# Late work moved to the end of VectorE's attention slot in a macaron block

## What is computed

```python
x = x + 0.5 * ffn(layernorm(x))
x = x + attn(layernorm(x))
x = x + 0.5 * ffn(layernorm(x))

def attn(x, Q, K, VO):                      # 16 heads, rank 64
    xq = einsum('btd,hrd->bthr', x, Q)
    xk = einsum('bud,hrd->buhr', x, K)
    p = softmax(einsum('bthr,buhr->bthu', xq, xk) / sqrt(128), axis=3)
    return einsum('bthu,bud,hde->bte', p, x, VO)

def ffn(x):                                 # 3 blocks, dequantized weights + LoRA
    h = x
    for blk in range(3):
        y = gelu(layernorm(linear(h, 2 * blk)) * gamma + beta)
        h = linear(y, 2 * blk + 1) + h
    return h
```

## Time and profile before

| what | us |
|---|---|
| median of 3 runs (lowest, highest) | 1020.96 (1019.09, 1021.09) |
| the profiled execution, its own time | 1021.44 |
| its span, first to last instruction | 1019.3 |
| TensorE busy in the span | 961.0 |
| VectorE busy | 887.4 |
| GpSimd busy | 826.2 |
| ScalarE busy | 808.5 |

### The profile page before, as it was taken

The page is one execution under the profiler, slowest core; times in us unless marked ns, Lnnn a source line. Parts: engine busy times, 40 slices in busy tenths (PEclk is TensorE's granted clock), DMA queues, the critical chain, the costliest instruction groups (busy, mean ns, idle before and its releaser), DMA issues.

```text
span 1019.3 us, 19252 instructions
## 1 busy us (share of the span) xinstructions
PE 961.0 (94%) x5892; PEld 499.6 (49%) x5892; DVE 887.4 (87%) x1782; ACT 808.5 (79%) x1343; POOL 826.2 (81%) x912
## 2 busy tenths in 40 slices
PE   4897799999999999999999999999999999999897
PEld 4664244444444444444444444444444444444675
DVE  7678998998999899989998999899989988995566
ACT  4875579878888888888888978897889788878674
POOL 2646389889898999899989998999889988899552
PEclk9998899999999999999999999999999999999999
DMA  9000323233222322222233223222222232321002
GB/s 245 1 2 0 83 60 63 57 64 64 55 60 60 64 62 63 63 63 63 63 63 63 63 62 64 57 63 57 62 58 63 57 66 62 65 57 27 2 1 83
DMA packets 71742, 59.87 MB, mean 59 GB/s; under 512 B 11168, under 2 KB 70560, under 8 KB 71648
## 3 DMA queue, kind: packets, MB, share of 16 engines
q1 hardware_dynamic: 71392, 58.31, 26.4%
q10 hardware_dynamic: 256, 0.39, 0.2%
HBM read 6.23 MB, written 2.10 MB: 8 GB/s over the span
## 4 chain that ended last, share of the span: by engine, by line
PE 71%; DVE 19%; issue 4%; ACT 3%; POOL 2%; DMA 1%; DVEq 0%; SPq 0%; ACTq 0%; POOLq 0%
PE ps L1156 9%; PE ps L1158 9%; PE ps L1157 9%; PE ps L1148 8%; PE ps L1149 8%; PE ps L1141 5%; DVE mcol L900 5%; PE ps L1086 3%; PE ps L1175 3%; PE ps L1133 3%; PE ps L1058 3%; PE ps L1171 2%; PE ps L1172 2%; DVE head_ops L911 2%; PE ps L1135 2%
## 5 line engine op out<-in xcount | busy, mean ns | idle before, releaser
L455 POOL TENSOR_TENSOR p_lo<-work_b,p_hi 128x1024 f16<-128x1024 f32 x256 | 539.8, 2129 | 76.3 <-ACT p_hi L610 74.0
L900 DVE TENSOR_REDUCE mcol<-ps 128x2 f16<-128x1024 f32 x256 | 301.0, 1220 | 0.7 <-PE ps L1141 0.6
L605 ACT ACTIVATE work_b<-ps,exp_scale 128x1024 f32<-128x1024 f32 x256 | 271.6, 1111 | 33.3 <-PE ps L1149 31.9
L610 ACT ACTIVATE p_hi<-work_b 128x1024 f16<-128x1024 f32 x256 | 256.1, 1055 | 0.0
L1148 PE MATMUL ps<-head_ops 128*128 128x512 f16 x512 | 195.0, 381 | 1.1 <-DVE mcol L900 1.1
L1156 PE MATMUL ps<-p_hi,xn_hi 128*128 128x512 f16 x512 | 194.8, 380 | 0.4 <-DVE pair_ops L889 0.4
L1149 PE MATMUL ps<-head_ops 128*128 128x512 f16 x512 | 194.9, 381 | 0.0
L1158 PE MATMUL ps<-p_lo,xn_hi 128*128 128x512 f16 x512 | 194.1, 379 | 0.0
L1157 PE MATMUL ps<-p_hi,xn_lo 128*128 128x512 f16 x512 | 194.1, 379 | 0.0
L464 POOL TENSOR_TENSOR x<-x,o_sb 128x512 f32<-128x512 f32 x128 | 162.7, 1271 | 6.5 <-DVE o_sb L928 2.1
L911 DVE STREAM_TRANSPOSE head_ops<-mcol 32x128 f16<-32x128 f16 x512 | 155.4, 303 | 9.3
(11 more groups left out here) (131 smaller groups left out, 1390.9 us busy)
## 6 DMA issues: line engine op xcount, KB each, us to landing
head_ops<-pair_ops SPq DMA_DIRECT2D x512, 64.0 KB, 2.0
head_ops<-pair_ops SPq DMA_DIRECT2D x128, 128.0 KB, 2.4
x<-x_dram SPq DMA_DIRECT2D x8, 256.0 KB, 6.1
out<-x SPq DMA_DIRECT2D x8, 256.0 KB, 2.6
vo_last<-wvo_dram SPq DMA_DIRECT2D x1, 1024.0 KB, 11.9
qk<-wq_dram SPq DMA_DIRECT2D x1, 512.0 KB, 5.3
qk<-wk_dram SPq DMA_DIRECT2D x1, 512.0 KB, 6.1
scl<-scales_dram ACTq DMA_DIRECT2D x8, 48.0 KB, 5.5
```

What stands on the lines that cost most here:

```text
L455: pool.tensor_tensor(p_lo[:, k % 2, rows, :], p32[:, k % 2, rows, :], p_hi[:, k % 2, rows, :], ALU.subtract).then_inc(plo_done, 1)
L605: nc.scalar.activation(p32[:, k % 2, 2 * a:2 * a + 2, :], s_ps[a], ACT.Exp, scale=exp_scale[:, 0:1]).then_inc(exp_done, 1)
L610: nc.scalar.activation(p_hi[:, k % 2, 2 * a:2 * a + 2, :], p32[:, k % 2, 2 * a:2 * a + 2, :], ACT.Copy).then_inc(phi_done, 1)
L900: nc.vector.tensor_reduce(mcol[:, pair % 2, :, t, 0], s_ps[t % 2], AX.X, ALU.max, negate=True).then_inc(max_red, 1)
```

## The change

One line moves. In VectorE's `slot(k)`, the call of `late(k)` stood between the two `reduce_max` and `y_low(k)`; it now stands at the end of the slot, behind `y_low(k)` and `k_low` or `q_low`. The other engines' programs are as they were.

```diff
--- before
+++ after
@@ -953,7 +953,6 @@
                 if -4 <= k < NH - 4:
                     for a in range(2):
                         reduce_max((k + 4) // 2, 2 * (k % 2) + a)
-                late(k)
                 if k == NH - 1:
                     seed(1, 0)
                     seed(1, 1)
@@ -970,6 +969,7 @@
                         k_low(pair, buf)
                     else:
                         q_low(pair, buf)
+                late(k)
 
             for k in SLOTS:
                 slot(k)
```

## The result

The changed kernel takes 1034.1 us (median, 1034.07 to 1035.61) against 1020.17 us for the kernel before, run beside it: ratio 1.0136, 95% interval 1.0122 to 1.0149, so 13.9 us slower. Slower was forecast, with 1039.0 and a range of 1031 to 1049. The profiled execution took 1035.61 us with a span of 1033.5, 14.2 more than the span before.

A forecast was written before the change was run, and what follows sets the result against it. TensorE was taken to set the pace. Removed `y_low` waits -14.2, readers +27.9, bn_stats +1.3 and seeds +2.6 sum to +17.6 us, on 1021.4 giving 1039.0 us; range 1031 to 1049.

The forecast's parts named there:

- What bounds it: Attention stage: TensorE sets the pace, busy 100.98 of 103 us at granted clock 1.00; only what makes it wait counts.
- Readers of late_ps, +27.9: `outputs` waits for moved step_x_half or split: 14 x 0.95, 6 x 0.96 and 6 x 1.47 us, +27.9.
- The two parts of the offset: Reader starts at +1.32 after the start of `y_low`; its result reaches TensorE 0.06 us after its end.
- Waits for y_low removed, -14.2: Third matmul of `outputs` (line 1175) no longer waits for `y_low` at 14 seeds: 13.3 and 0.93, booked -14.2 us.
- Seeds at the end, +2.6: A lone seed, 0.74 us, delays the second reduce_max; TensorE waits 0.32 in 8 slots, +2.6 us.
- The 2.05 end of the range: Upper end for the seed's first tensor_scalar at the slot's end, taken as 0.24 us with ends 0.24 and 2.05.
- the rival in which GpSimd still holds the seeds: GpSimd holds the ports by add_out or late p_lo; seeds cost 19.5 instead of 2.6, 1055.9 us; chance 0.08.
- as the order said: GpSimd's next instruction, the Newton step, needs the seed, so in queue order it issues nothing before it.
- bn_stats at the end, +1.3: bn_stats alone, 0.51 us, makes the second reduce_max late; TensorE waits 0.09 in 14 slots, +1.3 us.
- The waits of line 1148 for 900 that the forecast named as a sign: Sign in the list of waits: line 1148 waits for line 900, some 0.3 us at lone seeds.
- GpSimd and the ramp, nothing: GpSimd's longer seed wait has cover 1.3 us; late work in slots -3 to -1 is ±1.9; both booked at zero.

The follow-up runs named there:

- the bn_stats run: Against the kernel before, only bn_stats moved to the end of the slot, readers and seeds staying ahead of y_low: 1021.56 us, ratio 1.0007.
- the summing form: Against the kernel before, the seed's first tensor_scalar (line 774) also sums into a spare column, the second unchanged: 1017.29 us, ratio 0.9971.

## Why the prediction was right, point by point

- **What bounds it.** Right. TensorE's clock was granted at 1.00 in the batch looked at, before and after, and 13.1 of the 14.2 us between the profiled executions are there by slot 121, in the lengths of the slots. The fall of the clock behind the stage, 1.1, was not foreseen; it brings the time nearer to the forecast by luck.
- **Readers of late_ps, +27.9.** By starts 20 x 0.93 + 6 x 1.44 = 27.2. The two parts of the offset were each off and cancelled: the reader starts at +1.20 to +1.21 (the gap of 0.71 ahead of `row_max` does not exist ahead of other work), and its result needs 0.16, not 0.06, to start `outputs`. That the readers are the cause is shown by three runs: alone they give +21.9, read 0.6 us earlier they cost 0.33 instead of 0.93, and put ahead of bn_stats they lose the 0.51.
- **Waits for y_low removed, -14.2.** This is the term that was mis-sized most. I took the listed idle times (1.14, 0.88, 0.93). By starts the third matmul of `outputs` came 1.41 after the first (315.84, below, to 317.25) where 0.11 is usual, so 1.30 was lost, and 1.05 and 1.10 in the other kinds: 7 x 1.30 + 6 x 1.05 + 1.10 = 16.5. The run with the two tensor_scalar at the end takes just these waits away and measured 16.6, 16.2 by the slots.

```profile
315.84 0.22 PE L1171 MATMUL ps<-vo_hi,y_hi 128*128 128x129 f16 x1
```

- **Seeds at the end, +2.6.** Measured by starts about 2.1: 774 takes 0.17 rather than 0.24. The 2.05 end of the range and the rival in which GpSimd still holds the seeds did not occur; its queue did wait for the seed, as the order said.
- **bn_stats at the end, +1.3.** Measured 0.6: it costs 0.10 in the six slots that a turn follows, nothing in the others.
- **A wait I had not counted.** Five of the lone seeds, and those bn_stats, delay TensorE not through `reduce_max` but through its `late_turn`, which also waits for `scale_out` (line 1205). After the seed above, VectorE's `scale_out` is over at 431.33 (430.64 + 0.69), and TensorE's timeline goes on:

```profile
431.01 0.38 PE L1135 MATMUL ps<-xt_hi,w_lo 128*128 128x512 f16 x1
431.47 0.41 PE L1025 MATMUL ps<-ident,work_a 128*128 128x128 f32 x2
```

  Usually the turn follows line 1135 in 0.21 (469.26 to 469.47 before). Here it is 0.25 later, near the 0.32 I had for `reduce_max`, so the sum hid it. Where no turn is due, the two halves of `scores` come 0.10 and 0.19 late, 0.29 in all, against the 0.32 that I had put on the second half alone. The waits of line 1148 for 900 that the forecast named as a sign are not in the list from 130 to 955 us; they show only by starts. This is read from the traces; the bn_stats run agrees, and no run separated the two further.
- **GpSimd and the ramp, nothing.** Right for GpSimd: its wait for the seed rose by 14.4 us without a wait of TensorE. In the ramp `scores` of slot 1 starts at 126.21 instead of 126.32; from the stage's first `scores` that is 12.09 against 11.91, +0.18.

Sum by starts: -16.5 + 27.2 + 2.1 + 0.6 = 13.4, against 13.1 at slot 121 of the profiles (13.4 from the first `scores`) and 13.9 between the medians. The prediction's 17.6 was 3.7 above the latter and 4.2 above the sum by starts; of the 4.2, 2.3 is the term of `y_low`, 0.7 the readers, 0.7 bn_stats, 0.5 the seeds.

The four parts of this change have different signs. Taken together they cost 13.9 us; the one part that pays, cut so that each piece lies in a wait that exists, gives 16.6.

## What to carry to other kernels

When a block of work is moved in an in-order queue, list who waits for each instruction in it and how long before its next work; a block is seldom one thing, and here the seeds wanted to be late while the PSUM readers, with the next matmul of those banks waiting, had to be early. Work fits where the engine already waits, here 0.5 us ahead of `y_low`, and what overruns that is to be compared with the slack behind it, piece by piece. A rest that the moved work can't account for may be the granted clock: look at its rows before calling it scatter. Price a stall by the starts of the waiting engine's instructions against an undisturbed slot, not by its listed idle time.

## What the runs showed of the hardware

- A 128x4 tensor_scalar in float32 or int32 took 0.17 us with no p_lo of GpSimd under way. Issued during one, it ended some 0.03 us after it, unless less than its own 0.16 us was left: 1.02 to 1.52 us in the kernel before, 0.82 to 1.32 with the summing form ahead, 0.28 to 0.45 in the run with late work one instruction earlier. Of two on end the second took 0.17 where no further p_lo was under way, and 2.05 at the first seed, where the next p_lo was under way (126.44 to 128.57). The same operation with an accumulator took 0.16 us during p_lo, with 0.08 more for the read of the accumulator.
- Listed idle of TensorE was 0.16 or 0.17 us less than the time lost, in each of the waits examined (0.77 to 0.93, 1.28 to 1.44, 1.14 to 1.30, 0.88 to 1.05, 0.93 to 1.10).
- From the end of a VectorE instruction to the start of a matmul that waits for it: 0.15 us ahead of `outputs`' first matmul (all 26 waits of the changed kernel; the rounded rows give 0.16), 0.06 ahead of its third.
- Matmuls of the second FFN that start every 0.43 us at a granted clock of 1.00 started every 0.85 us while it was at 1.2 GHz, for 3.4 us (971.0 to 974.5 of the changed kernel).
